# Two-layer cross-attention and mixture-of-experts kernel: blocks 2 and 3 of the first layer made in another order, their units built one step behind their raw copies

## What is computed

```python
def _L0_xattn_ref(query, key, value, Wq, bq, Wk, bk, Wv, bv, Wo, bo):
    ...
    q = (query @ Wq.T + bq).reshape(B, S, H, D).transpose(0, 2, 1, 3)
    k = (key @ Wk.T + bk).reshape(B, S, H, D).transpose(0, 2, 1, 3)
    v = (value @ Wv.T + bv).reshape(B, S, H, D).transpose(0, 2, 1, 3)
    cos, sin = _rope_cache(S, D, q.dtype)
    q = _apply_rope(q, cos, sin)
    k = _apply_rope(k, cos, sin)
    scores = jnp.einsum('bhsd,bhtd->bhst', q, k) / math.sqrt(D)
    attn = jax.nn.softmax(scores, axis=-1)
    out = jnp.einsum('bhst,bhtd->bhsd', attn, v)
    out = out.transpose(0, 2, 1, 3).reshape(B, S, E)
    return out @ Wo.T + bo
```

## Time and profile before

| what | value |
|---|---|
| timed runs (3) | 983.6, 984.75, 990.06 us; median 984.75 |
| profiled execution, its own time | 988.88 us |
| its span, first to last instruction | 987.1 us |
| mean granted clock of PE | 0.958 |
| PE busy | 878.9 us, 89% of the span |
| DVE, ACT, POOL busy | 67%, 49%, 38% |
| layer 0's attention steps 3 to 11 | 62.28 to 137.90 us |

### The profile page before, as it was taken

How to read it: one execution, slowest core, us unless ns; L and a number is a source line. 1 busy time by engine, 2 the same in 40 slices (tenths; PEclk the granted TensorE clock), 3 DMA queues, 4 the chain that set the end, 5 groups by cost and what they waited for, 6 DMA issues and landing times.

```text
span 987.1 us, 21017 instructions
## 1 busy us (share of the span) xinstructions
PE 878.9 (89%) x7941; PEld 768.0 (78%) x7941; DVE 656.6 (67%) x1367; ACT 483.6 (49%) x809; POOL 379.9 (38%) x390
## 2 busy tenths in 40 slices
PE   5688888974899999999956899989899999999997
PEld 4577776752789999999944788867788888888886
DVE  6876776540457777777758556766966666666666
ACT  3666568510336677676634665685222222222221
POOL 4353344067106888888750322220212212121210
PEclk9799999985899999999988999999999999999999
DMA  7029020024236888888661000110010100010002
GB/s 207 23 67 284 29 71 2 1 86 151 90 124 167 235 226 231 237 230 222 173 154 44 24 2 2 35 34 1 17 33 16 32 16 32 16 32 16 16 1 86
DMA packets 46112, 85.43 MB, mean 87 GB/s; under 512 B 6240, under 2 KB 33120, under 8 KB 45920
## 3 DMA queue, kind: packets, MB, share of 16 engines
q0 software_dynamic: 14784, 46.44, 17.4%
q1 hardware_dynamic: 31264, 38.09, 12.8%
HBM read 63.73 MB, written 20.79 MB: 86 GB/s over the span
## 4 chain that ended last, share of the span: by engine, by line
PE 71%; DVE 10%; ACT 8%; issue 6%; POOL 3%; DMA 2%; DVEq 0%; SPq 0%; ACTq 0%; POOLq 0%
PE bank L1398 38%; PE bank L1434 12%; PE bank L1493 5%; PE bank L1607 3%; PE bank L1654 2%; PE bank L1583 2%; ACT prob L730 2%; PE bank L1688 2%; PE bank L1664 1%; DVE low_f L1220 1%; DMA ctx_raw<-in_ctxT 1%; DVE xres L1091 1%; DVE xT_lo L907 1%; PE bank L1387 1%; PE bank L1459 1%
## 5 line engine op out<-in xcount | busy, mean ns | idle before, releaser
L1101 DVE TENSOR_TENSOR hid<-bank,act_sb 128x512 f32<-128x512 f32 x88 | 60.8, 691 | 147.0 <-ACT act_sb L661 127.0
L661 ACT ACTIVATE act_sb<-bank 128x512 f32<-128x512 f32 x88 | 52.5, 597 | 204.8 <-PE bank L1398 164.2
L1398 PE MATMUL bank<-xT_hi,w_hi 128*128 128x512 f32 x352 | 141.3, 402 | 7.9 <-issue 4.8
L1398 PE MATMUL bank<-xT_hi,w_lo 128*128 128x512 f32 x352 | 141.4, 402 | 6.8 <-issue 6.6
L1398 PE MATMUL bank<-xT_lo,w_hi 128*128 128x512 f32 x352 | 141.5, 402 | 5.7 <-issue 5.7
L1091 DVE SCALAR_TENSOR_TENSOR xres<-bank,gate,xres 128x256 f32<-128x256 f32 x320 | 132.7, 475 | 1.4 <-PE bank L1434 1.4
L404 POOL TENSOR_TENSOR w_hi<-w_raw,zero_col 128x768 fp32r<-128x768 f32 (+1 forms) x20 | 31.9, 1595 | 243.7 <-PE bank L1434 239.0
L1398 PE MATMUL bank<-xsT_hi,w_hi 128*128 128x256 f32 x368 | 105.7, 287 | 2.2 <-DVE xsT_lo L1058 1.5
L1434 PE MATMUL bank<-w_hi,hid_hi 128*128 128x256 f32 x352 | 102.1, 290 | 5.8 <-DVE hid_lo L1106 5.8
L472 POOL DMA_INDIRECT summed<-y_sb,tile_to x46 | 94.9, 2064 | 27.1 <-issue 12.7
L1434 PE MATMUL bank<-w_lo,hid_hi 128*128 128x256 f32 x352 | 101.1, 287 | 3.0 <-issue 3.0
(11 more groups left out here) (207 smaller groups left out, 2196.9 us busy)
## 6 DMA issues: line engine op xcount, KB each, us to landing
w_raw<-in_fw SPq DMA_DIRECT2D x18, 384.0 KB, 3.0
sorted_x<-empty_row SPq DMA_DIRECT2D x2, 2967.0 KB, 19.8
xs<-sorted_x SPq DMA_DIRECT2D x23, 258.0 KB
ctx_raw<-in_ctxT SPq DMA_DIRECT2D x8, 512.0 KB, 4.7
summed<-empty_row SPq DMA_DIRECT2D x1, 2304.0 KB, 26.7
xres<-in_x SPq DMA_DIRECT2D x4, 512.0 KB, 6.9
xn_all<-summed SPq DMA_DIRECT2D x4, 512.0 KB, 5.8
out_x<-xres SPq DMA_DIRECT2D x4, 512.0 KB, 3.0
```

Of the source, the lines that this page charges most:

```text
L661: nc.scalar.activation(act_sb[:, r, :], bank[2 * r + 1][:], ACT.Silu).then_inc(f["act"], 1)
L1101: nc.vector.tensor_tensor(hid[:, r, :], bank[2 * r][:], act_sb[:, r, :], ALU.mult).then_inc(f["hid"], 1)
L1398: last = nc.tensor.matmul(dst, lh, rh, start=(i == 0), stop=(i == len(pairs) - 1))
```

## The change

In `PLAN` of layer 0 the items of blocks 2 and 3 stand in another order, with three of them in steps 3 and 7 and none in step 11:

```diff
-                 3: ((2, X0), (2, K0)), 4: ((2, X1), (2, K1)), 5: ((2, Q0), (2, Q1)), 6: ((2, V0), (2, V1)),
-                 7: ((3, X0), (3, K0)), 8: ((3, X1), (3, K1)), 9: ((3, Q0), (3, Q1)), 10: ((3, V0),), 11: ((3, V1),)},
+                 3: ((2, K0), (2, X0), (2, X1)), 4: ((2, Q0), (2, Q1)), 5: ((2, K1), (2, V0)), 6: ((2, V1),),
+                 7: ((3, K0), (3, X0), (3, X1)), 8: ((3, Q0), (3, Q1)), 9: ((3, K1), (3, V0)), 10: ((3, V1),)},
```

The half of a unit is no longer u % 2 but `half_of(item)`, with the same values as before. All units of blocks 2 and 3, and as before Q1 of block 1, are built and rotated in the step behind the one that makes them, after `lowest(b+1)` on DVE and after `three_parts(b+1)` on POOL:

```diff
+        def same_half(l, m, item):
+
+            earlier = [p for p in UNIT_ORDER[l][:unit_no(l, m, item)] if half_of(p[1]) == half_of(item)]
+            return earlier[-1] if earlier else None
+
+        def built_late(m, item):
+
+            return m >= 2 or (m, item) == (1, Q1)
+
+        def late_units(b):
+            return [p for p in items_of(0, b - 1) if p[1] in (K0, K1, Q0, Q1) and built_late(*p)] if b else []
...
                         if l == 0:
-                            for m, item in items_of(l, b - 1):
-                                if item == Q1:
-                                    made_item(m, item)
+                            for m, item in late_units(b):
+                                unit_build(m, item)
```

The waits for the buffers go by the unit that was last in the same half. K1 is now the last unit of its block, so what its build waits for is the pair of copies of Q1 of the same block (`q1set`); `rotate` of a K also waits for the turned scores that still use its place in `k_full`:

```diff
-                    if u >= 2:
-                        if q:
-                            dve.wait_ge(a["kk"], 2 * m + r + 1)
+                    if last:
+                        if last[1] in (K0, K1):
+                            dve.wait_ge(a["kk"], 2 * last[0] + r + 1)
                         else:
-                            dve.wait_ge(a[f"q{r}set"], 2 * m)
+                            dve.wait_ge(a[f"q{r}set"], 2 * last[0] + 2)
...
                     if item in (K0, K1):
+                        if m >= 2:
+                            pool.wait_ge(a["turn"], BLK * (m - 1))
```

On ACT, the normalization of block 3 goes from step 5 to step 7, and in steps 6 and 10 both pairs of `q_half` copies stand inside the exponentials:

```diff
-                        if b in ((3, 5), (1, 4))[l]:
-                            normal(2 * l, 2 + b // 4)
+                        if b in ((3, 7), (1, 4))[l]:
+                            normal(2 * l, 2 + b // 4 if l else 2 + b // 7)
...
-                        if l == 0 and (b // BLK + 1, Q0) in items_of(l, b - 1):
+                        if l == 0 and b == 2:
+                            unit_out(1, Q0)
+                        if l == 0 and b in (6, 10):
                             unit_out(b // BLK + 1, Q0)
                         exponential(b, 2)
+                        if l == 0 and b in (6, 10):
+                            unit_out(b // BLK + 1, Q1)
                         exponential(b, 3)
...
-                        if l == 0 and (b // BLK + 1, Q1) in items_of(l, b - 1):
-                            unit_out(b // BLK + 1, Q1)
+                        if l == 0 and b == 2:
+                            unit_out(1, Q1)
```

More of the change, by code:

```diff
@@ L240, in unit_no, with half_of, units_now @@
             return UNIT_ORDER[l].index((m, item))
+        def half_of(item):
+            return int(item in (K1, Q1))
+        def same_half(l, m, item):
[5 more added lines that the diff above has]
+            return [p for p in items_of(0, b - 1) if p[1] in (K0, K1, Q0, Q1) and built_late(*p)] if b else []
+        def units_now(b):
+            return [p for p in items_of(0, b) if p[1] in (K0, K1, Q0, Q1) and not built_late(*p)]
         def slot_bank(l, m, item):
@@ L553, in _ @@
                     if l == 0:
-                        for m, item in items_of(l, b):
-                            if item in (K0, K1, Q0):
-                                rotate(m, item)
+                        for m, item in units_now(b):
+                            rotate(m, item)
                     if l == 0 and b == 11:
@@ L716, in raw_out @@
                 def raw_out(m, item):
-                    u = unit_no(l, m, item)
+                    u, last = unit_no(l, m, item), same_half(l, m, item)
                     act.wait_ge(a["proj"], u + 1)
-                    if u >= 6:
-                        act.wait_ge(a["rope"], 3 * (u - 2) + 2)
-                    nc.scalar.activation(unit_raw[:, u % 2, :], bank[unit_bank(l, m, item)][:],
+                    if last[0]:
+                        act.wait_ge(a["rope"], 3 * unit_no(l, *last) + 2)
+                    nc.scalar.activation(unit_raw[:, half_of(item), :], bank[unit_bank(l, m, item)][:],
                                          ACT.Copy).then_inc(a["raw"], 1)
@@ L1160, in unit_build @@
                     u = unit_no(l, m, item)
-                    r, q = u % 2, item in (Q0, Q1)
+                    r, q, last = half_of(item), item in (Q0, Q1), same_half(l, m, item)
                     if l == 1 and item != Q0:
@@ L1265, in attend @@
                         for m, item in items_of(l, b):
-                            if l == 1 or item != Q1:
+                            if l == 1 or item not in (K0, K1, Q0, Q1) or not built_late(m, item):
                                 made_item(m, item)
```

26 lines of the change are left out of this document (12 added, 14 removed).

## The result

| | median, us | timed runs |
|---|---|---|
| before | 984.84 | 4 (983.6 to 990.06) |
| after | 997.34 | 4 (997.08 to 999.51) |

The ratio is 1.0116, 95% interval 1.0089 to 1.0142: the changed kernel is 12.5 us slower. The forecast was +6.1 us and 990.9, its range ended at 995.0. The direction was right, the size half of what came. The profiled execution took 997.19 us, span 995.4.

The account below looks back on a forecast made before the run. TensorE (PE), busy for 89% of the span, was taken as the bound, so order matters only where PE waits. The terms of steps 3 to 11 sum to +6.1 us: 984.75 + 6.1 = 990.9 us, range 983.0 to 995.0.

Parts of the forecast that it names:

- The nine steps: Steps 3 to 11 of layer 0's attention loop, each one pass over b: 81.7 us together after the change, against 75.62.
- rival (c): Behind the loop, at the expert weights' split and router stage, half of the delay is absorbed: 987.8 us; chance 0.11.
- The chain through `q1set`: In steps 6 and 10 K1's build waits for ACT's q_half pair of Q1; +1.3 and +3.3 us.
- steps 6 and 10: Attention loop: 11.2 us against 9.94 (+1.3) and 12.2 against 8.94 (+3.3), with PE idle for 4.7 and 5.8.
- Steps 3, 4 and 8: Attention loop: +0.25 us for one X item more in the first, +0.35 in each of the other two.
- X1's wait: In steps 4 and 8 the turned scores wait 0.77 us for the low part of X1.
- Step 5's term of -0.5: Attention loop: DVE, with both Q builds between maxima and output, sets 8.96 us against 9.47.
- Rival (a): Q1's q_half pair ends before the maxima of steps 6 and 10, the waits go: -3.1, 981.7 us; chance 0.15.
- steps 5 and 9: Attention loop: 8.96 us each with both Q builds at 2.09; -0.5 against 9.47 and -0.25 against 9.21.
- step 7: Attention loop: 8.72 us against 6.78 (+1.95), 1.6 of it the lowered clock after PE's idle, bounds 1.5 and 2.7.
- step 11: Attention loop: 7.3 us against 7.93 (-0.6), its clock loss already there before, its end set by DVE.
- Rival (b): Clock low for 5.34 us in steps 7 and 11, step 5's idle back elsewhere: +9.7, 994.5 us; chance 0.14.

Follow-up runs that it names:

- e2: The changed kernel, but POOL's rotation of Q0 in blocks 2 and 3 waits until DVE has built Q1; ratio 1.0091 to the kernel before.
- e4: The changed kernel with X0 and X1 ahead of K0 in steps 3 and 7; one execution, no time given; steps 4 and 8 fell by 0.89 us each.
- e6: The changed kernel with products that nobody reads in PE's idle time of steps 5, 6, 9 and 10; ratio 1.0057 to the kernel before.
- e1: The changed kernel with both q_half pairs of copies ahead of the first exponential on ACT in steps 6 and 10; ratio 1.0012 to the kernel before.
- e7: The changed kernel, but Q0 of blocks 2 and 3 is built in the step of its raw copy (4 and 8); ratio 1.0031 to the kernel before.
- e5: The changed kernel again without an edit, on another chip; ratio 1.0107 to the kernel before.
- e9: The kernel before with 8 products that nobody reads on PE behind the last work of step 10; ratio 0.9969 to the kernel before.
- e3: The changed kernel with the edits of e1 and e2 together; ratio 0.9986 to the kernel before.
- e8: The changed kernel with the edits of e1, e4 and e7 and block 3's normalization back in step 5; ratio 0.9923 to the kernel before.
- e10: e8 with 8 products that nobody reads on PE behind the last work of step 10; ratio 0.9922 to the kernel before.

## Why the prediction fell short, point by point

**Right.** The nine steps are the whole matter, and what stands behind them passes a shift on (rival (c) falls: 35.28 and 35.29 us). The chain through `q1set` sets steps 6 and 10: without the clock they took 11.0 and 12.46 or 12.47 in e2, e4 and e6, against 11.2 and 12.2, and e1 takes them away. Steps 3, 4 and 8 came within 0.17 us, and X1's wait at 0.67 against 0.77. Step 5's term of -0.5 was worked out rightly for DVE without POOL: e2 has 8.94 for its 8.96. Rival (a) is what e1 made by hand: Q1's pair over before the maxima end. Its 7.6 and 8.4 for steps 6 and 10 came out at 7.95 and 8.75, but its gain of 3.1 us at 0.1 in the steps: steps 5 and 9 took 2.0 of it, steps 6 and 10 0.7 and steps 3, 4 and 8 0.4.

**The step that failed: steps 5 and 9 at 8.96, with both Q builds at 2.09 each.** Both took 9.97. The builds were priced as if POOL were not there, but as soon as the first build's shuffle is over (81.60 + 0.74) the rotation of Q0 starts, at 82.42, and meets the second build. This price could be read before: in block 1, where two builds also stand back to back, the kernel before has the pair already. DVE and POOL of the kernel before:

```profile
43.36 0.73 DVE L1181 SCALAR_TENSOR_TENSOR qk<-unit_raw,bias_col,rope_tab 128x512 f32<-128x512 f32 x1
44.01 1.76 DVE L1181 SCALAR_TENSOR_TENSOR rope_b<-unit_raw,bias_col,rope_tab 128x512 f32<-128x512 f32 x1
```

```profile
43.54 1.68 POOL L503 TENSOR_TENSOR k_full<-qk,rope_b 128x512 f32<-128x512 f32 x1 [0.20 <-DVE rope_b L1188]
```

I took the price of a build from one that stood alone, and not from the place that looks like the new one. It is worth +2.0 us of the 6.6 us by which the steps missed (88.31 against 81.7). The rows fit an exclusive hold: the rotation starts at 82.42 while the first product runs until about 82.88, and is 0.43 longer than alone; it ends at 84.12, and the product that started at 82.88 ends 0.54 behind it, 0.2 less than the 0.74 that it takes alone. The Trainium skill, "SBUF — State Buffer" (Who interferes with whom), states just this: a VectorE instruction with two SBUF inputs and a GpSimd instruction that reads SBUF take turns, and the second to start is blocked until the first is over. The trace agrees, but for these 0.2 us.

**The term that was mis-sized: the clock, put at 1.6 us more in step 7 and at nothing more elsewhere.** I gave the lowered clock to one more step. It came to three more. Steps 6 and 10 lost 1.5 us each to it (12.51 against 11.0, 13.97 against 12.46), after an idle of 2.09 us which is itself the collision's: with the forecast's 8.96 it would have been 1.06, and e2 with 1.06 and e7 with none show a full clock in both as long as PE works. Against the terms of 11.2 and 12.2 that is +3.1. In step 7 the lowered clock cost 2.4 to 2.8 us (9.61 and 10.00 against e6's 7.19), near the upper bound I had (2.7) and not the row of this loop: +0.9. That price is not fixed by the length of the idle: e2, after 4.56 us of it, took 8.81, which is 1.6 over 7.19 and the forecast's own figure; e4, after the same 4.56, took 9.46. In the changed kernel and e4 the clock fell while PE still idled (step 6 above has 0.81 in its idle part), in e2 only within the scores of step 7. In step 11 the forecast missed not the clock but what hangs on it: PE's output projection came late, and DVE's residual, which the forecast had straight behind the statistics, waited 0.18 us for it, so that 1.85 us went by from the statistics to the residual where 1.58 were counted: +0.3. In all the lowered clock cost 1.4 us there (7.77 in e5 against e6's 6.36) and 1.55 in the kernel before (7.93 against e9's 6.38). DVE in step 11 of the changed kernel:

```profile
145.78 1.39 DVE L913 BATCH_NORM_STATS2 stats<-xres 128x6 f32<-128x256 f32 x4
147.09 0.36 DVE L916 BATCH_NORM_AGGREGATE meanvar<-stats 128x2 f32<-128x6 f32 x4
147.63 0.42 DVE L1258 TENSOR_TENSOR xres<-bank,xres 128x256 f32<-128x256 f32 x1 [0.18 <-PE bank L1709]
```

With 0.4 in steps 3, 4 and 8 this is 2.0 + 3.1 + 0.9 + 0.3 + 0.4 = 6.7, the whole miss but rounding. How much of it one execution shows is in part chance: e4 has the same collision and the same idle ahead of steps 6 and 10, and took 3.0 us less in them. Rival (b) came closest, 994.5 us, with step 5's idle "at a place with no slack" and a longer lowered clock in steps 7 and 11, but not for the reason that made the difference.

The range was too narrow for one reason: it held the clock's bounds for step 7 alone. That an idle of 2.44 us had lowered the clock once should have asked of every step in which PE's idle came out near 2 us; a build 1 us dearer in steps 5 and 9 was enough to reach it.

**A reading that was wrong, without a part in the miss.** The 1.38 us that PE lacks in step 5 of the kernel before were put down to the weighed sum's wait for the maxima. The trace has them inside the products of `low_row`, 1.37 us in which nothing is shown to end the wait:

```profile
79.28 0.42 PE L1614 MATMUL bank<-low_row,pick 32*128 32x128 bf16 x14
81.07 0.23 PE L1614 MATMUL bank<-low_row,pick 32*128 32x128 bf16 x2 [1.37 <-issue]
```

In steps 4, 8 and 9 the wait is where the prediction has it (1.34 us ahead of the weighed sum in step 4).

**Still open.** Why the idle of 2.08 to 2.09 us lowered the clock in steps 6 and 10 of the changed kernel, e1 and e5 but not in e4. And what the pauses inside the products of `low_row` are: 1.37 us in step 5 of the kernel before and 1.10 in e9, 1.20, 0.93 and 0.38 in step 7 of e3, e8 and e10. In the kernel before and e9 they stand behind the fourteenth of the sixteen products, in e3, e8 and e10 behind the tenth, and all of them in steps in which the DMAs move 254 to 313 GB/s; most such steps have none, and neither question was put to an experiment. The table's steps are of one execution each, and the timed medians need not hold all of its lowered stretches: e1 and e5 differ by 13.3 us in their steps and by some 9 in their ratios.

## What to carry to other kernels

Price a moved instruction at the place in the trace that looks like its new one, with the same neighbour on the other engine, and not where it stood alone. An idle of PE can have two prices, its own length and a stretch at half clock behind it (here, ahead of these steps, behind every idle of 1.89 us and more but two of 2.08 and 2.09 in e4, and behind none up to 1.83); it was the second that I had sized worst, and its size varies from one execution to the next. To learn whether a step is long by its waits or by its clock, fill the idle time with products that nobody reads: if it gets shorter, it was the clock (at least in part). And an order whose waits have been named can be mended: four small moves took the changed order from 1.1% slower to 0.8% faster.

## What the runs showed of the hardware that was not expected

- A VectorE product of two SBUF operands beside a GpSimd subtraction took 1.76 to 1.79 us instead of 0.74 (seven times in the profiles of before, after and e5), the GpSimd one 1.68 to 1.71 instead of 1.27; with the order forced in steps 5 and 9 (e2) both lengthenings were gone there.
- PE's granted clock fell after an idle of 2.08 or 2.09 us in both steps of three executions (the changed kernel's two, after and e5, and e1), with scores of 1.41 or 1.58 us or, where these still took 1.17, behind them; in e4 it stayed full behind the same two idles. After 1.06 (e2, e3) it never fell. After 4.44 to 4.56 us of idling it cost 1.6 to 2.8 us in the step behind (8.81 in e2 to 10.00 in e5, against 7.19).
- Added work made two kernels faster: 58 products in the idle time of the changed kernel (e6), 8 in that of the kernel before (e9, 3.0 us by its ratio).
